# Two cross-attentions and two quantised feed-forward layers on one core: gapped rows for VectorE's rounding steps, small operations split by tiles, two jobs moved to GpSimd, and weight loads moved forward

## What is computed

```python
x = x + _L0_xattn_ref(_layernorm(x), ctx_1024, Wq, bq, Wk, bk)      # softmax(q k^T), no mask; x times the attention
x = x + _L0_ffn_ref(_layernorm(x), w_norm, w_gv, w_out)             # 8-bit activations, ternary weights, silu gate
x = x + _L1_xattn_ref(_layernorm(x), ctx_1024, mask, Wq, Wk, Wv, Wo)  # 16 heads on 8 pairs, masked softmax
x = x + _L1_ffn_ref(_layernorm(x), gate_w, up_w, down_w, scales)    # weights rounded to fp8 (e4m3), then fp32

# second layer
h = x * rsqrt(mean(x * x) + EPS) * w_norm
step = maximum(max(abs(h)), EPS) / 127          # per row; round(h / step) goes into the product
# third layer, per batch and head
scores = where(mask, q @ k.T / sqrt(128), -inf)
attn = nan_to_num(softmax(scores), nan=0.0)     # a batch without any valid key adds nothing
# fourth layer
wq = w.astype(float8_e4m3fn).astype(float32)
```

## Time and profile before

| | us |
|---|---|
| median of 3 runs | 313.3 (310.11 to 313.8) |
| the profiled execution | 312.58 |
| its span, first to last instruction | 310.5 |
| TensorE busy in it | 293.6 |
| VectorE busy | 260.9 |
| ScalarE busy | 253.7 |
| GpSimd busy | 218.5 |

### The profile page before, as it was taken

One profiled execution on the slowest core, in us unless ns is written; L12 is line 12 of the kernel. 1 busy time (PEld: TensorE's weight loads), 2 busy tenths in 40 slices (PEclk: granted clock), 3 DMA queues, 4 the chain that ended last, 5 costly groups with the idle time before them and its releaser, 6 DMA issues.

```text
span 310.5 us, 6396 instructions
## 1 busy us (share of the span) xinstructions
PE 293.6 (95%) x1980; PEld 259.9 (84%) x1992; DVE 260.9 (84%) x713; ACT 253.7 (82%) x603; POOL 218.5 (70%) x290
## 2 busy tenths in 40 slices
PE   3968999999999999999999999999999999999994
PEld 2755487798989998979889999999988999899884
DVE  3959999999999999889999986997768897675665
ACT  2398995598999998979999899778899999855460
POOL 3558864556998578999879998886678798952001
PEclk9979999999999999999999999999999999999999
DMA  7996032001326548885878756537645647200103
GB/s 223 367 381 199 35 101 70 1 8 30 93 47 189 157 138 251 220 212 139 228 210 226 199 144 174 161 108 219 182 144 148 179 143 211 68 3 0 36 1 101
DMA packets 54609, 44.59 MB, mean 144 GB/s; under 512 B 11696, under 2 KB 45104, under 8 KB 54576
## 3 DMA queue, kind: packets, MB, share of 16 engines
q1 hardware_dynamic: 54016, 43.93, 49.0%
q10 hardware_dynamic: 560, 0.26, 0.3%
HBM read 27.01 MB, written 15.20 MB: 136 GB/s over the span
## 4 chain that ended last, share of the span: by engine, by line
PE 59%; DVE 20%; DMA 8%; issue 5%; SPq 4%; ACT 2%; DVEq 0%
PE pb L2016 41%; DMA block_room<-blocks 5%; PE pb L2279 5%; PE pb L2314 4%; DMA wraw<-in_wgvT 3%; DVE blocks L1581 3%; SPq L442 2%; DVE sm L1564 2%; PE pb L2130 2%; PE pb L2091 2%; PE pb L2076 2%; DVE wraw L1455 2%; DVE step L1601 1%; PE pb L2227 1%; DVE q_lo L1551 1%
## 5 line engine op out<-in xcount | busy, mean ns | idle before, releaser
L667 POOL TENSOR_TENSOR tp_lo<-tp,pT_hi 128x512 fp32r<-128x512 f32 x54 | 70.0, 1311 | 15.1 <-ACT pT_hi L993 14.8
L981 ACT ACTIVATE sm<-sm,smin 128x256 f32<-128x256 f32 x128 | 63.6, 501 | 4.7 <-DVE smin L1564 4.4
L1564 DVE CUSTOM_DVE_ANT_0 sm<-pb,mask_all 128x256 f32<-128x256 f32 x128 | 47.3, 418 | 5.6 <-PE pb L2016 5.5
L1581 DVE STREAM_TRANSPOSE blocks<-sm 128x1024 f32<-128x1024 f32 x27 | 33.5, 1240 | 7.4 <-DMA block_room<-blocks 7.0
L2016 PE MATMUL pb<-ctx_hi,q_hi 128*128 128x256 f32 x128 | 38.1, 298 | 1.1 <-DVE q_lo L1551 0.6
L662 POOL TENSOR_SCALAR sm<-sm,srec 128x256 f32<-128x256 f32 x64 | 30.5, 488 | 10.4 <-DVE srec L1570 10.4
L2016 PE MATMUL pb<-xT_hi,m_hi 128*128 128x256 f32 x128 | 37.3, 292 | 0.3 <-DVE xT_lo L1540 0.3
L2016 PE MATMUL pb<-n_hi,oT_hi 128*128 128x256 f32 x128 | 37.1, 290 | 0.2 <-DVE oT_lo L1595 0.2
L2016 PE MATMUL pb<-xT_hi,m_lo 128*128 128x256 f32 x128 | 36.2, 283 | 0.0
L2016 PE MATMUL pb<-xT_lo,m_hi 128*128 128x256 f32 x128 | 36.2, 283 | 0.0
L2016 PE MATMUL pb<-ctx_lo,q_hi 128*128 128x256 f32 x128 | 36.2, 282 | 0.0
(11 more groups left out here) (195 smaller groups left out, 943.0 us busy)
## 6 DMA issues: line engine op xcount, KB each, us to landing
block_room<-blocks SPq DMA_DIRECT2D x108, 128.0 KB, 2.8
tp<-block_room SPq DMA_DIRECT2D x54, 256.0 KB, 3.0
w_raw<-in_w SPq DMA_DIRECT2D x4, 576.0 KB, 4.6
wraw<-in_wgvT SPq DMA_DIRECT2D x4, 512.0 KB, 8.4
wraw<-in_woutT SPq DMA_DIRECT2D x2, 512.0 KB, 9.3
out<-xb SPq DMA_DIRECT2D x4, 256.0 KB, 2.2
xa<-in_x SPq DMA_DIRECT2D x3, 256.0 KB, 4.5
xb<-in_ctxT SPq DMA_DIRECT2D x2, 256.0 KB, 5.1
```

What stands on the lines that cost most here:

```text
L667: g.tensor_tensor(tp_lo[:, z, c, :], tp[:, z, c, :], as_f32(pT_hi[:, c, :]), ALU.subtract).then_inc(pT_lo_pool, 1)
L981: a.activation(sm[:, n % 2, k, :], sm[:, n % 2, k, :], ACT.Exp, bias=smin[:, n % 2, k:k + 1], scale=-1.0, accum_out=ssum[:, n % 2, k:k + 1 ...
L1564: v.tensor_tensor_reduce(out=sm[:, n % 2, k, :], in0=bank(passing_bank("s", 2 * n + h))[:, (k % 2) * S:(k % 2 + 1) * S], in1=mask_all[:, b ...
L1581: v.transpose(blocks[:].rearrange("p g k b -> p k g b"), sm[:, n % 2, :, :].rearrange("p k (g b) -> p k g b", b=32)).then_inc(blocks_done, 1)
```

## The change

1. sum8 becomes three rows of 96 values with a pitch of 97. The exponent is written there (no longer into step8), the step is read from there and written to step8, and GpSimd's four operations read or write sum8 in the same shape.
2. The operations on two columns (nmean, ve, and all of scaled() but the reciprocal) become two operations on one column each; the products with rstd become operations with a pointer to a column, and the max with EPS goes into the one before it.
3. ctx_lo's two halves and the mask's values are made by GpSimd. The reduction over the mask goes; some_key(b) is made in masked(n) of the batch's second step from its least scores. masked(0, 0) and eighth(0) wait for the first of the mask steps, added3(b) for the flag of its batch.
4. SP issues the loads of the second, third and fourth quarter together, behind turn_hidden(3).

```diff
-        sum8 = tile(ctx, "sum8", [P, PIECE])[:]
+        sum8 = tile(ctx, "sum8", [P, 3, PIECE // 3 + 1])[:, :, 0:PIECE // 3]
...
+        def thirds(piece):
+            return piece.rearrange("p (a n) -> p a n", a=3)
...
-                    sp.wait_ge(mask_step, 2)
+                    sp.wait_ge(mask_step, 1)
...
             turn_hidden(2)
             turn_hidden(3)
+            eighth(1)
+            eighth(2)
+            eighth(3)
             blocks_written(3)
...
             blocks_written(7)
-            eighth(1)
             blocks_read(7)
...
             blocks_written(12)
-            eighth(2)
-            eighth(3)
             blocks_read(12)
...
+            def context_low(n):
+                pool.wait_ge(ctx_hi_done, n + 1)
+                g.tensor_tensor(ctx_lo[:, ctx_part(n)], ctx_raw[:, ctx_part(n)], as_f32(ctx_hi[:, ctx_part(n)]), ALU.subtract).then_inc(ctx_lo_done, 1)
+
+            def mask_values():
+                pool.wait_ge(ld_mask, 16)
+                g.tensor_scalar(mask_all[:, 0:B, 0:S], mask8[:], -MASKED, MASKED, ALU.mult, ALU.add).then_inc(mask_step, 1)
...
-                raw = w8_raw[:, n * PIECE:(n + 1) * PIECE]
+                raw = thirds(w8_raw[:, n * PIECE:(n + 1) * PIECE])
...
-                g.tensor_tensor(sum8, raw, step8, ALU.add).then_inc(sum8_done, 1)
+                g.tensor_tensor(sum8, raw, thirds(step8), ALU.add).then_inc(sum8_done, 1)
...
-                g.tensor_tensor(w8r[:, n * PIECE:(n + 1) * PIECE], sum8, step8, ALU.add).then_inc(w8_done, 1)
+                g.tensor_tensor(thirds(w8r[:, n * PIECE:(n + 1) * PIECE]), sum8, thirds(step8), ALU.add).then_inc(w8_done, 1)
...
-                v.tensor_scalar(nmean[:, sl], mv[:, sl, 0], -1.0, None, ALU.mult)
+                for t in range(sl.start, sl.stop):
+                    v.tensor_scalar(nmean[:, t:t + 1], mv[:, t, 0:1], -1.0, None, ALU.mult)
...
-                scale_next(v.tensor_tensor(hmax[:, sl], hmax[:, sl], rstd[:, 1, sl], ALU.mult))
-                scale_next(v.tensor_scalar(hstep[:, sl], hmax[:, sl], EPS, 1.0 / 127.0, ALU.max, ALU.mult))
+                each = [slice(t, t + 1) for t in range(sl.start, sl.stop)]
+                for one in each:
+                    scale_part(v.tensor_scalar(hmax[:, one], hmax[:, one], rstd[:, 1, one], EPS, ALU.mult, ALU.max))
+                dve.wait_ge(scale_step, scale_count[0])
+                for one in each:
+                    scale_part(v.tensor_scalar(hstep[:, one], hmax[:, one], 1.0 / 127.0, None, ALU.mult))
+                dve.wait_ge(scale_step, scale_count[0])
                 scale_next(v.reciprocal(hrec[:, sl], hstep[:, sl]))
-                scale_next(v.tensor_tensor(hqs[:, sl], hrec[:, sl], rstd[:, 1, sl], ALU.mult))
+                for one in each:
+                    scale_part(v.tensor_scalar(hqs[:, one], hrec[:, one], rstd[:, 1, one], None, ALU.mult))
+                dve.wait_ge(scale_step, scale_count[0])
...
-            def mask_values():
-                dve.wait_ge(ld_mask, 16)
-                v.tensor_reduce(mask_all[:, 0:B, S], mask8[:], AX.X, ALU.max).then_inc(mask_step, 1)
-                dve.wait_ge(mask_step, 1)
-                v.tensor_scalar(mask_all[:, 0:B, 0:S], mask8[:], -MASKED, MASKED, ALU.mult, ALU.add).then_inc(mask_step, 1)
...
-                    dve.wait_ge(mask_step, 2)
+                    dve.wait_ge(mask_step, 1)
+                if n % PAIRS == 1 and h == 0:
+                    dve.wait_ge(sm_done, 4 * n)
+                    v.tensor_scalar(mask_all[:, b, S:S + 1], smin[:, 0, 0:1], 0.5 * MASKED, None, ALU.is_lt).then_inc(mask_step, 1)
...
-                v.tensor_scalar(step8.bitcast(I32), w8_raw[:, n * PIECE:(n + 1) * PIECE].bitcast(I32), 0x7F800000, None,
+                v.tensor_scalar(sum8.bitcast(I32), thirds(w8_raw[:, n * PIECE:(n + 1) * PIECE]).bitcast(I32), 0x7F800000, None,
                                 ALU.bitwise_and).then_inc(exp8_done, 1)
                 dve.wait_ge(exp8_done, 2 * n + 1)
-                v.tensor_scalar(step8, step8, FP8_LEAST, FP8_STEP, ALU.max, ALU.mult).then_inc(exp8_done, 1)
+                v.tensor_scalar(thirds(step8), sum8, FP8_LEAST, FP8_STEP, ALU.max, ALU.mult).then_inc(exp8_done, 1)
...
                 dve.wait_ge(attn_ps, PAIRS * (b + 1))
+                dve.wait_ge(mask_step, b + 2)
```

More of the change, by code:

```diff
@@ L669, in eighths @@
             def eighths(n):
-                raw = w8_raw[:, n * PIECE:(n + 1) * PIECE]
+                raw = thirds(w8_raw[:, n * PIECE:(n + 1) * PIECE])
                 pool.wait_ge(exp8_done, 2 * n + 2)
-                g.tensor_tensor(sum8, raw, step8, ALU.add).then_inc(sum8_done, 1)
+                g.tensor_tensor(sum8, raw, thirds(step8), ALU.add).then_inc(sum8_done, 1)
             def eighths_out(n):
                 pool.wait_ge(sum8_done, n + 1)
-                g.tensor_tensor(sum8, sum8, step8, ALU.subtract).then_inc(step8_done, 1)
+                g.tensor_tensor(sum8, sum8, thirds(step8), ALU.subtract).then_inc(step8_done, 1)
                 pool.wait_ge(step8_done, 2 * n + 1)
-                g.tensor_scalar(step8, sum8, FP8_OVER, 0.0, ALU.mult, ALU.mult).then_inc(step8_done, 1)
+                g.tensor_scalar(thirds(step8), sum8, FP8_OVER, 0.0, ALU.mult, ALU.mult).then_inc(step8_done, 1)
                 pool.wait_ge(step8_done, 2 * n + 2)
-                g.tensor_tensor(w8r[:, n * PIECE:(n + 1) * PIECE], sum8, step8, ALU.add).then_inc(w8_done, 1)
+                g.tensor_tensor(thirds(w8r[:, n * PIECE:(n + 1) * PIECE]), sum8, thirds(step8), ALU.add).then_inc(w8_done, 1)
             def rows4(b):
@@ L702, in _ @@
             base(0)
+            context_low(0)
             rows1(3)
@@ L712, in _ @@
             integers(1)
+            context_low(1)
             ternary_out(4)
@@ L715, in _ @@
             rows3(0)
+            mask_values()
             base(2)
@@ L1388, in _ @@
             v.memset(minus_round[:], -ROUND).then_inc(filled, 1)
-            def context_low(n):
-                dve.wait_ge(ctx_hi_done, n + 1)
-                v.tensor_tensor(ctx_lo[:, ctx_part(n)], ctx_raw[:, ctx_part(n)], as_f32(ctx_hi[:, ctx_part(n)]), ALU.subtract).then_inc(ctx_lo_done, 1)
             def values_low(c):
@@ L1409, in stats @@
                 dve.wait_ge(mv_done, bn_count[0])
-                v.tensor_scalar(nmean[:, sl], mv[:, sl, 0], -1.0, None, ALU.mult)
+                for t in range(sl.start, sl.stop):
+                    v.tensor_scalar(nmean[:, t:t + 1], mv[:, t, 0:1], -1.0, None, ALU.mult)
             def variances(sl, done):
-                v.tensor_scalar(ve[:, 0, sl], mv[:, sl, 1], EPS, None, ALU.add).then_inc(done, 1)
+                for t in range(sl.start, sl.stop):
+                    ins = v.tensor_scalar(ve[:, 0, t:t + 1], mv[:, t, 1:2], EPS, None, ALU.add)
+                ins.then_inc(done, 1)
             def stats1(b):
@@ L1460, in second_stats @@
                 stats(xa, sl)
-                v.tensor_scalar(ve[:, 0, sl], mv[:, sl, 1], EPS, None, ALU.add)
-                v.tensor_scalar(ve[:, 1, sl], mv[:, sl, 1], 1.0 + EPS, EPS * EPS, ALU.mult, ALU.add).then_inc(ve2_done, 1)
+                for t in range(sl.start, sl.stop):
+                    v.tensor_scalar(ve[:, 0, t:t + 1], mv[:, t, 1:2], EPS, None, ALU.add)
+                    ins = v.tensor_scalar(ve[:, 1, t:t + 1], mv[:, t, 1:2], 1.0 + EPS, EPS * EPS, ALU.mult, ALU.add)
+                ins.then_inc(ve2_done, 1)
             def centred(b):
@@ L1478, in _, with scale_part, scale_next @@
             scale_count = [0]
-            def scale_next(ins):
+            def scale_part(ins):
                 scale_count[0] += 1
                 ins.then_inc(scale_step, 1)
+            def scale_next(ins):
+                scale_part(ins)
                 dve.wait_ge(scale_step, scale_count[0])
@@ L1488, in scaled @@
                 dve.wait_ge(rstd2_done, b + 1)
-                scale_next(v.tensor_tensor(hmax[:, sl], hmax[:, sl], rstd[:, 1, sl], ALU.mult))
-                scale_next(v.tensor_scalar(hstep[:, sl], hmax[:, sl], EPS, 1.0 / 127.0, ALU.max, ALU.mult))
+                each = [slice(t, t + 1) for t in range(sl.start, sl.stop)]
[5 more added lines that the diff above has]
+                dve.wait_ge(scale_step, scale_count[0])
                 scale_next(v.reciprocal(hrec[:, sl], hstep[:, sl]))
-                scale_next(v.tensor_tensor(hqs[:, sl], hrec[:, sl], rstd[:, 1, sl], ALU.mult))
+                for one in each:
+                    scale_part(v.tensor_scalar(hqs[:, one], hrec[:, one], rstd[:, 1, one], None, ALU.mult))
+                dve.wait_ge(scale_step, scale_count[0])
                 if b == 0:
                     dve.wait_ge(wmean_done, 1)
-                v.tensor_scalar(gsc[:, sl], hstep[:, sl], wmean[:, 0:1], None, ALU.mult).then_inc(gsc_done, 1)
+                for one in each:
+                    ins = v.tensor_scalar(gsc[:, one], hstep[:, one], wmean[:, 0:1], None, ALU.mult)
```

(4 more changed lines are left out.)

## The result

The changed kernel takes 318.16 us (median of 4 runs, 314.94 to 318.38), the kernel before beside it 313.24. The ratio is 1.0153, with a 95% interval of 1.0104 to 1.0202: some 1.5% slower, where 311.6 was predicted and the range ended at 316.0. The profiled execution took 318.38 us, its span 316.1. Now and then an execution of any of these kernels is slower, at a lower granted clock; the ratios leave such executions out, the medians count them.

A forecast was written before the change was run, and what follows sets the result against it. TensorE, busy 293.6 of 310.5 us, was taken as the bound, so only its waits could shrink. Terms -2.0 - 0.3 + 1.1 + 0.3 + 0.3 - 0.4 = -1.0 took 312.58 to 311.6 us; range 307.2 to 316.0.

The forecast's parts named there:

- The steps, -2.0 us: Quantised pieces' two step operations on VectorE: gapped rows stop them standing still for GpSimd, saving TensorE 2.0 us (0 to 3.1).
- the last of the signs of being wrong: TensorE waiting for the same operands behind other VectorE work, showing that the stops were not what made them late; no size.
- wout, +1.1 us: Near 50 us: ctx_lo's second subtraction on GpSimd delays wout and TensorE's first product with it; +1.1 us (0.5 to 1.9).
- The start, +0.3: Up to 47 us, where VectorE sets the time: two split scaled() cost 2 x 0.52, gain one stop; +0.3 us (0 to 0.7).
- The loads, +0.3 (0 to 1.8): Three quarter loads ahead of the block writes issued at 91.81 delay their landing and the next transposition; 0.3 us on TensorE.
- Small operations before 76.32, -0.3: Last scaled() before TensorE's wait at 76.32: single-column operations lose the stop behind GpSimd; net -0.1 to -0.5, taken as -0.3 us.
- -0.4 after 190 us: TensorE's waits after 190 us, of the same kind as those shown, shrink by 0.4 us (0 to -0.8).
- Rival three: GpSimd becomes the bound because gapped rows slow its four operations per piece; some 322 us, chance 0.07.
- Rival one: Gaps don't take the step operations out of the faster mode, they still stop and gain nothing; 314.0 us, chance 0.09.
- Rival two: TensorE's waits for VectorE go altogether and the wout delay is covered, 0.5 of it staying; 308.0 us, chance 0.18.
- the 0.04 for loads that hold the blocks for longer: Chance of 0.04 that the quarter loads hold the block writes for longer than forecast; no time given.

## Why the prediction was wrong

- **The steps, -2.0 us: right at the products, wrong in the sum.** The operations run at 442 and 453 ns in the median (429 and 477 at most were predicted) and never stop, and the four late products regain 1.91 us. The step that failed is the one from the late products to the whole time: that what is regained at a product stays regained, as if nothing else were as late. (The term has a lower bound of 0 for that case, without a row for it; and the last of the signs of being wrong came true: TensorE waits for q_lo and oT_lo behind other work of VectorE.) VectorE's stops were one hindrance; behind them stood the circle of transposition, block write and landing. Its 7.0 us lead the view of VectorE's waits of the kernel before, and the chain from 214 to 240 us consists of it; the prediction uses neither. With one buffer the gapped rows alone make +0.6%, and with a second buffer beneath them -0.5% (0.9960 to 0.9909, whose intervals overlap a little). Where the forecast looked for time in VectorE's stops, the runs show it in the circle: 14.8 us more of VectorE's waiting there, 2.46 us lost at three products, and 1.0153 turned into 1.0054 by a second buffer.
- **wout, +1.1 us: right.** TensorE waits 1.3 us there, the second product comes at once behind the first, and the second half of ctx_lo costs 1.2 by the table of the halves. GpSimd's subtraction took 1.71 instead of 1.29 us.
- **The start, +0.3: a cost was left out.** The split itself came out as sized: 0.51 us at the first scaling, 0.33 regained at the next, 0.2 up to wout. What is missing is the first half of ctx_lo, 1.0 to 1.2 us. I forgot the rule that I had drawn from the earlier trace rows one paragraph before: a GpSimd operation that is moved is one more for a VectorE operation to stand still behind. Another 0.9 us of the profiled execution's lateness is not the change's.
- **The loads, +0.3 (0 to 1.8): mis-sized, by the same blind spot.** The delayed landing holds the transposition, and q_lo stands behind it in VectorE's list: 1.5 us of TensorE's waiting, and "later by" grows by 1.88 at the product at 103.85, just over the upper end of 1.8 (by 1.3 from 53.59 on, as 0.6 had been regained between). I named what queues behind the wait and then took it as covered.
- **Small operations before 76.32, -0.3: right in size** (79.41 against 76.32, 0.27 us regained there), and of no weight that is seen: the runs with and without the split are alike within their intervals.
- **-0.4 after 190 us: wrong sign.** At 199.54 and 245.97 us 0.68 and 0.89 us were lost, by the circle.
- **Rival three** (gapped rows slow GpSimd) fell: of GpSimd's four operations two took less (806 and 809 ns, now 768 both) and two the same within 10 ns. **Rival one** fell with the step operations' rows. **Rival two** needed the waits for VectorE to go; they changed their cause. None of the rivals named the block writes as the bound; nearest is the 0.04 for loads that hold the blocks for longer, which has no price.

The Trainium skill's rule on two columns per cycle (page "VectorE: DVE Perf Modes", section "What auto-detection actually checks") held: with 3 rows against 288 columns all 32 operations took 0.41 to 0.46 us, where 0.26 and 0.31 had been the best, and none stopped. The stop at 73.86 from which the prediction argued is of another kind, an operation with two inputs; for the step operations it is this result that shows it.

## What to carry to other kernels

Before making an engine faster, look at what it waits for, not only at who waits for it: a circle through one buffer (make, write out, landing, make again) that shows a few microseconds of waits can become the bound as soon as the engine arrives earlier, as it did here. In a list that is worked off in order, the operand behind the blocked instruction is what the next engine misses, so a wait is priced by what stands behind it. And work that is moved to GpSimd is to be checked against the VectorE operations that will run beside it, and beside what it moves back in GpSimd's list, since these may stand still until it ends.

## What the runs showed of the hardware

- The same write of 128 KB took 2.3 and 2.4 us (medians) in two profiles of the kernel before, where VectorE came 1.1 to 2.2 us after the landing that frees its buffer, and 2.9 to 3.1 in four with gapped rows, where it mostly came within 0.4, in the same stretch of the program. The cause of the difference is open.
- VectorE and GpSimd hold each other up both ways: the subtraction on GpSimd took 1.27 us at 29.62, where VectorE's ternary operation stood still (1.69 us, 0.68 before), and 1.71 at 49.77, where one was running as it began.
- The granted clock was 0.75 in the mean from 20 to 30 us of the changed kernel's execution: 0.50 (1.2 GHz) from 20 to 24 and 1.00 (2.4 GHz) from 26 on, after TensorE had waited 3.15 us for wpart. In the kernel before it was 0.50 from 18 to 20 and 1.00 from 22 on, after a wait of 2.40. "Later by" was 1.40 near 27.3 us and back at 0.91 by 28.76, so little of the result hangs on it.

```profile
20.00:30.00 10.00, 9.71 (x48) 8.28 (x47) 8.54 (x22) 8.56 (x19) 8.55 (x12) 0.75 0.64 213
```
